# Four fused layers on one core: layer 2's scores four row strips at a time, layer 3's condition as a narrow product, one order for the whole program

## The chip, the cores and the metric

The kernel runs on one core of one Trainium2 chip, as a single launch. The metric is the device time of that launch in microseconds (us), lower is better. The core has five engines with a queue each: PE (matrix products and transposes), DVE (vector), ACT (scalar, exponentials), POOL (a second, slower vector engine) and SP (here it only starts transfers). Everything is float32. One float32 product shows in the trace as two MATMUL records, each with a LDWEIGHTS record of its own.

## The reference

Thirty-two batches of 128 tokens with 128 features pass through four layers, one after the other:

- Layer 0: adaptive layer norm, attention with 16 heads of 64, and a 512-wide MLP with GELU, both gated.
- Layer 1: RMS norm with FiLM, attention with one head of 128, and an MLP.
- Layer 2: adaptive layer norm, attention with 16 heads of 8, and an MLP, both gated.
- Layer 3: a graph attention. Its first product is what this change touches:

```
row_zero = v.sum(-1) == 0
q_exp = where(row_zero, 0, q[:, None, :])          # q: the condition of the batch, 128 numbers
self_feat = concat([v, q_exp], -1) @ W_self.T + b_self
for d in range(2):                                  # two directions, 16 heads of 8, keys: the first 20 nodes
    aff = (q_d . k_d) * scale, masked by adj, + label bias;  softmax;  weighted sum; output product
out = v + relu(output)
```

In layer 2, scores are `einsum('bqhd,bkhd->bhqk', Q, K)` with 8 features per head, softmax over the 128 keys.

## The kernel before

The 32 batches are worked in NG = 8 groups of G = 4 batches, so that a tile of 4 x 128 = 512 columns fills one of the eight PSUM banks. A group passes through four parts, each a Python generator that yields after every step: `front` (layer 0's attention, 76 steps), `mid` (layer 0's MLP and all of layer 1), `back` (layer 2) and `last` (layer 3). Each part has one set of SBUF tiles, so it works on one group at a time, while the other parts work on other groups. Every engine runs the same step lists and does its own share of each step.

What decides which step is next on an engine is a written order, `ORDERS`: a string of letters for each engine, one letter per step, made beforehand. `weave` walks the string and advances the generator of that letter. Before the change there are three orders: "head" (329 steps: groups 0 to 2 fill the pipeline), "steady" (170 steps, walked NG - 4 = 4 times, with the front of group it+3, mid of it+2, back of it+1 and last of it) and "tail" (348 steps: the remaining parts drain). PE's order also deals the banks: `Phase` walks it and gives each result that a step `begins` the bank that has been free longest; a bank is held from the step that begins the result to the step that lists it in `ends`. At run time PE waits on a semaphore until the bank's last reader is done.

The steps that the change touches:

- `S2` (layer 2, steps 0 to 7 of a group, two for each batch). The 16 heads of a batch are 4 units ("A", u), each a row strip: 32 of the 128 partitions hold the 8 features of 4 heads. The moving operand `km` holds the keys with the other heads' features set to zero, so one product of 32 rows, 128 columns of weights and 2 x 128 moving columns gives two heads. Step k computes units 2k and 2k+1 (line 1142), two strips into two banks. DVE then takes each unit's row maximum (line 1451), ACT the exponentials of unit 2k in `S2` and of 2k+1 in `E2` (line 947), and PE transposes the results in `T2` and `T2'` (line 1150). `V2` (line 1160) multiplies by the values, with four column strips side by side.
- `adj` (layer 3): PE transposes the edge sums of the second direction into a bank (line 1182); DVE copies the condition of the four batches from `condT` to `gcond` (line 1518), waits for that copy, and builds the mask and bias.
- `sum3`: PE sums the features of each token over the partitions (line 1017, weights `ones`); DVE turns this into `qx`: the condition where the sum is not zero, else 0, for 4 x 128 columns (line 1537).
- `self3`: PE computes `W_v x3 + W_q qx`, two 512-column products into one bank, the second of which waits for DVE's `qx`; DVE adds the bias (line 1381).

```
elif what == "self3":
    linear(P, "self3", [(w3[:, 0, :], x3T[:, :]), (w3[:, 1, :], qx)], after=["sum3"])
```

SP has its own hand-written sequence of waits and loads: the next group's input for the front (`load_norm`), the input again for the residual (`load_res`), the edge masks (`load_edges`, five transfers) and the stores.

Of the kernel before, what the change touches and what calls it, by code (L numbers as in the profile page):

```python
# [133 lines left out]
def end_steps():  # L134
    steps = [Step("adj", 0, ["adj"], ["adj"]), Step("sum3", 0, ["sum3"], ["sum3"]),
             Step("self3", 0, ["self3"], ["self3"]), Step("qk3", 0, ["q3_0", "q3_1", "k3"], ["q3_0", "q3_1", "k3"])]
    for s in range(NU3 + 5):
# [10 lines left out]
        if s < NU3:  # L148
# [8 lines left out]


STEPS = {"F": front_steps(), "M": mid_steps(), "B": back_steps(), "E": end_steps(), "A": front_steps(), "Q": front_steps(),
         "U": mid_steps(), "L": front_steps(False), "N": mid_steps(), "C": back_steps(), "D": back_steps(), "G": end_steps(),  # L160
         "H": end_steps(), "I": end_steps()}
STEP_NS = {"F": {"qk": 1720, "T": 440, "T'": 440, "S": 1000, "v": 900, "E": 300, "a": 1000, "I": 100, "stat": 300, "unit": 300, "turn": 450,
                 "o": 860, "y": 500},
           "M": {"stat": 1700, "unit": 1400, "turn": 1700, "up": 1900, "down": 1900, "back": 1500, "qk1": 1800, "v1": 1200,
                 "A1": 1500, "E1": 2500, "T1": 1000, "a1": 1200, "o1": 1500},
           "B": {"stat": 1700, "unit": 1400, "turn": 1700, "up": 1900, "down": 1900, "back": 1500, "kq2": 1900, "v2": 1200,
                 "S2": 1300, "T2": 1000, "T2'": 1000, "E2": 1000, "V2": 1300, "o2": 1800, "y2": 1500, "xt": 800},
           "E": {"adj": 1700,
                 "sum3": 1500, "self3": 1900, "qk3": 2500, "u3": 2000, "y3": 1500}}
STEP_NS.update({x: STEP_NS[kind] for kind, like in (("F", "AQL"), ("M", "UN"), ("B", "CD"), ("E", "GHI")) for x in like})  # L170

# [6 lines left out]
def edge_slot(i):  # L178
# [12 lines left out]
    "head": {  # L191
        "PE": (
            "AAAAAAAAAAAAAAAAAAAAAAAAAAAAAAAAAAAAAAAAAAAAAAAAAAAAAAAAAAAAAAAAAAAAAAAAAAAQAQUUQQQQUQQQQQQQQQUQUQQU"
            "UQQQUQQQUUQQUQQQQQUQQUUUQQQQQQQUQQUQQQQQQQUQQQUQQQQQUQQQUQUUQQQQQUQFFUQFQFQQQBQQQFQFFFFBFFFFMMFFMFBF"
            "FFFBMFBMBBMMBBBBFFBFBBFMFBFFFFFFBMBBMFBBFBMBFFBBFFFFBMBBFMMFFMFBFBMBFMBFFFMBBMFFBBBMFBBFFBFBFMFFFFBM"
            "BFBBFFBMFMFFBFFFFBFMFFFBFBFBB"),
        "DVE": (
            "AAAAAAAAAAAAAAAAAAAAAAAAAAAAAAAAAAAAAAAAAAAAAAAAAAAAAAAAAAAAAAAAAAAAAAAAAAAAQQUQQUQQQUQQUUUQQQQQQQQQ"
            "UQQQQUUQQQUQQUQQQUQUUQQQQQUQQQQQQQUQQQUQQUQQQUQQQUQUQUUQQQQQUQQQQQQQQFFUFQQQQQFQQFFFFFMBFMFFFBFFMMBF"
            "FFBFMBFBMFBFBBMBBBFFFMBBFMFFFFFBFBBFBMBBFBMBFBFBFFFMBFBBMMFBFFMBFFMBFMBBFFFMBMFBFBBBBFBMFBFFMFFBFFFB"  # L200
            "FFBBMFFMMBBFFFFBFFFFFBFBMFFBB"),
        "ACT": (
            "AAAAAAAAAAAAAAAAAAAAAAAAAAAAAAAAAAAAAAAAAAAAAAAAAAAAAAAAAAAAAAAAAAAAAAAAQQAQQQQQQAQQAAQQUQQUUUQUQQQQ"
            "QQQQUUQUQUQUQQQQQQUUQUUUQQQQUQQQQQQQQQQQQQQQUQQUQQUQQUQUQQUQUUUQQQQFQFQQFQQQFQBQQFFQFFFFMFFBBFMFFFFF"
            "FFMBMMBBBFFBBBBMBFFMFBBFFFFBFBBFFBFBFMBBBFFBMMFBFMFBFMMBBFMMFFBFBMFMMFFBFFBBBFBBFBFBBBMBFFMFMFFBFMMM"
            "FBFFFBFFFFFMBFFFFBFBFFBBFFBBB"),
        "POOL": (
            "AAAAAAAAAAAAAAAAAAAAAAAAAAAAAAAAAAAAAAAAAAAAAAAAAAAAAAAAAAAAAAAAAAAAAAAAAAAQQAQQUQQQQUUUUQQQQQQQQQQU"
            "UQUQQQQQQUQQQQQUUQUQQUUQUUQQUQQUQQQQQQQQQQQQQQQQUQQQUUUQQQQUFFQQQFQQQQFUQFQFFQQQQQQFUMBBMFMFMFMFMFBF"
            "FFBBBFBFFBBFBBFBFFMFBBMFBFFMFFFFFFFMBBMBBBBFFMFBBBFFBFFMMFFBFBFBBBMBMBFFMFBFBFFBFBBFMMBFMFBBFFFMFFFF"  # L210
            "BFFFBBBMFFMMFFBBFFFBMFFFFBBBB"),
    },
    "steady": {
        "PE": (
            "MFFFEBMFFFFBEBFBBMEBFFEBBBMEMEBBMFFBMFFEBFFBFFBMFFBFFBMBFFFBEBBFFFBFMFFBBEFBFBFMFEBFFFBMBMBMBFFMFFFF"
            "EBFMFFFFBMBEBBMFBFFFFBFFMFFFFBEMBFFBFFEMFFFFBMMBBFFFFBEBEMBMBFFBFBFEBE"),
        "DVE": (
            "MFBFMFBFBFEFFEFBBEBBMEBMEFMBBBMEFFFBBFMFBFEFFBFMFFBBFFBBBMFBFBFFBFEFFFFMEBFBBFFMFEBMFFFBBMBMBFFFMFMF"
            "BEFFEFFFFFBMBBMBFBFBFMFFBFFBFEFFMFFBFFMEFFFFMBEBFBMFFBFBMBMFFFEFBEBBBE"),
        "ACT": (  # L220
            "MBFEFFEBMMFFEEFBFBBFFEBFBBBMMBBFFFBFBFMFBMFBFBMEFFBFBFFMMFEFEBBBFFFFFFMBBBEFBFBFFEFFBFMBBBBFMFMFMFFF"
            "BEFMFFMFBBEBBBFMBFFMFFFFBFFFFFFBFEMMFBFEBFFFFMBMEEFMBEBBFBBFBFBFEMFBFF"),
        "POOL": (
            "MFEFEBBFFMBEFBBFFBMBFFEBBFBFFFBBFMEBFMFBFFBFBBEEBFFFFBMBMBMEFFMMBBBBFFBFFEFFBFFFFMFMBFBBFEFFFMMFMFFM"
            "BEBFFBEMFBBBFBFFFFMFFBBFBFFFFMFFFEFFFFFFEMMMMFFEEFFFBBFEFMEBFBBBBBBMBB"),
    },
    "tail": {
        "PE": (
            "BBLEMLLLLLLLBEMMBLBLBEBBBMEBMEBBLBMBLLLBMLELBLBLEMLBLMLBBBBELLBBEEBMBMBEBBEMLBLEMLLLMLBLELBLMLLLBLBM"
            "LBLMEBLBBLLLBMMLLLMBLEBLLLLEBLBBLLBMELLLLMBBLMBLBLLBBLMLLMLLLLCLLLLLCGGCGCCGNCNCNGCCGCNCNNCNGCCGNCCC"  # L230
            "NCCNNCCGNCCNCNGNCGCNCCNCCNGNCCCGCCGCCNCNGGCCGCNCNCCCCNNCGCCCCHDDDHDDDHDDHHDDDDHDDHDDDDDDDDHDHDDDDDDD"
            "DDHDDDDDDHDHDHDHDHDDHDDDHDDDDHIIIIIIIIIIIIIIIIII"),
        "DVE": (
            "BLBLMLEMLEBLLLMMLLBBBLBBEBBEMBEBBMLBBLLMLLEBLLBBLBELLLMMBBLBMEBLBEEBMBEBBBEMLLBELBBLLMMLLLLMELLEMLLB"
            "LLEBBBLBBBLMBLMLLMLMLBLLLLLEBBLBMLELBLLBLLLMBBLLLLBBLBMLMLLMLLLLLLLCGCGNCGCCGNCCNCGCNGCCCNCNNCGNCNCC"
            "CNCCGNCGCNCCGNNGNCNCGCCNCCNCCNGGCCCCNGCCCCNGCNGCCCCNCGCCNCCNCDDDHDHDDDHDDHDDHDDDHHDDDDDDDDHDHDDDDDDD"
            "DDDHDDDDHDHDDHHDDHDDHDDDHDHDDDIIIIIIIIIIIIIIIIII"),
        "ACT": (
            "BELMMLBEMLLLLLELBBLBLBBBBMMBEBEBBMBLEMLMMBLLMLBLELBLBEBLLBBLMLBLBEEBBBEBBBLEMBMMELLLLLMBBELLBLLLLMLL"
            "MMLBBLMLEBBBBLLLBLMLELBELBLLLBLBLEMLBLLLLBBMLBMBMBLLLLLLLBLMCLLLLLLLCGNGNCGGCCNCGGCCCNNCCCCNCNGCNCNC"  # L240
            "NCGCCGNCCNCCNNGGNCNCCCCNCCGCNNGCCGCNCCGCGCCCNNCCNGCCNCNGCCCCCDDDDDDDHHDDDHDDDHHHHDDHDDDDDDDDHDDDDDDD"
            "DDHDDDHDDDHDDHDDDDHDHHDDHDDDHDIIIIIIIIIIIIIIIIII"),
        "POOL": (
            "BBELMMLLELLLLBLLMMBBMLBBLBBBEMBBELBLMBBBBLBEEBBLBMLLEMBEBLLBMELLEBBBMLBEBMELLLELLMLLLLBLLBMBMLLMBBLE"
            "BLEMBMLLLBLMBLLLBMELLBBLLLBLLBBLMEMLBBMMLBLLLMLBLBLLLLLLLLLLLLLLBBCNNEGNGCGCCCCCCCGCCCGCCNNNCCGGNNNG"
            "NCCCGNNCNNCCCCGGNCNCCCCCNCNGNCCNGCCCGCCCGCCCCGCNCNCGNCNCCCNCDDGDDDDHHDHDHDHDDDDHDHDDDDDDDDHDHDDDDDDD"
            "DDHDDDDDDDHHDHHDDDDDDHHHDDDDDHIIIIIIIIIIIIIIIIII"),
# [8 lines left out]
def order_pairs():  # L256
# [18 lines left out]

    for a, b in ("AU", "UM", "QM", "UB", "LN", "MN", "MC", "BC", "ND", "CD", "EG", "BG", "GH", "CH", "HI", "DI"):
        follow(a, b)
# [25 lines left out]
class Phase:  # L303
# [3 lines left out]
    def __init__(self, banks, orders, turns=1, prefer=range(8)):  # L307
# [18 lines left out]
        for b in range(8):  # L326
            banks.dealt[b] += turns * self.per[b]
# [1334 lines left out]
```

## Time and the profile before

| | |
|---|---|
| median of 3 runs | 1239.77 us (1237.17 to 1240.85) |
| the profiled execution | 1240.78 us, of which the span from first to last instruction is 1239.0 us |
| mean granted PE clock | 0.946 of full |
| PE busy | 1110.0 us (90%) |
| DVE busy | 879.8 us (71%) |
| ACT busy | 772.8 us (62%) |
| POOL busy | 434.2 us (35%) |

A busy time is the union of the records of an engine. PE's two records for one product overlap their neighbours, so the mean duration of one is more than what it adds to the stream; the distance from start to start tells that. One pass of "steady" takes 134.6 us (a four-record product of line 1036 in the chain starts at 414.27, 548.90, 683.54 and 818.18 us).

### The profile page before, as it was taken

Reading aid. Unit: us, or ns where it says so; the run is one execution under the profiler, and the core shown is the slowest. Engines: PE = TensorE matmul, PEld = TensorE weight load, DVE = VectorE, ACT = ScalarE, POOL = GpSimd, SP = SyncE. Lnnn points to the kernel's source line nnn. Section 1 sums busy time; section 2 is a strip of 40 time slices with the busy share of each in tenths; the row PEclk is TensorE's granted clock in tenths of the full one; section 3 lists DMA queues with packets and bytes.
Section 4 is the critical chain, followed back from the end, with each engine's and each line's share of the span. In section 5 each row is a group of like instructions: output and inputs, shape, how many; then the busy total and the mean of one; then the engine's idle time right before and its main releaser. Section 6 shows DMA issues by size and latency. Waiting matters only on the chain.

```text
span 1239.0 us, 24134 instructions
## 1 busy us (share of the span) xinstructions
PE 1110.0 (90%) x8411; PEld 748.2 (60%) x8411; DVE 879.8 (71%) x2510; ACT 772.8 (62%) x2888; POOL 434.2 (35%) x599
## 2 busy tenths in 40 slices
PE   5889989989999999999999999998989977879865
PEld 4655755665567656775667656765666545646533
DVE  3456656775888688987799688877786478656655
ACT  1646557874688648873787468863866546726622
POOL 1322323332254333541445225432453234214313
PEclk9999999999999999999999999998979998886695
DMA  8000000001000100000000100010000100010000
GB/s 246 2 10 10 10 1 1 10 10 31 1 10 10 31 10 10 1 28 20 9 3 11 39 1 10 2 31 9 10 2 1 38 1 1 1 38 1 1 9 9
DMA packets 21822, 20.98 MB, mean 17 GB/s; under 512 B 1143, under 2 KB 20296, under 8 KB 21448
## 3 DMA queue, kind: packets, MB, share of 16 engines
q1 hardware_dynamic: 18536, 15.26, 4.4%
q10 hardware_dynamic: 3168, 4.19, 1.1%
q8 instruction: 69, 1.13, 0.4%
q14 instruction: 49, 0.40, 0.1%
HBM read 17.35 MB, written 2.10 MB: 16 GB/s over the span
## 4 chain that ended last, share of the span: by engine, by line
PE 63%; DVE 24%; ACT 7%; POOL 3%; issue 2%; DMA 1%; POOLq 0%; DVEq 0%; ACTq 0%
PE bank L1017 9%; PE bank L1036 7%; PE bank L1024 6%; PE bank L1142 5%; PE bank L1041 4%; PE bank L1074 4%; PE bank L1084 4%; PE bank L1150 3%; PE bank L1059 3%; PE bank L1068 3%; PE bank L1011 3%; PE bank L1232 2%; ACT prob_space L947 2%; PE bank L1221 2%; ACT fprobs L883 2%
## 5 line engine op out<-in xcount | busy, mean ns | idle before, releaser
L771 POOL TENSOR_TENSOR fprobs<-fprobs,frinv 128x512 f32<-128x512 f32 x128 | 132.4, 1039 | 282.5 <-DVE frinv L1327 282.2
L883 ACT ACTIVATE fprobs<-bank,fnegmax 128x128 f32<-128x128 f32 x512 | 180.8, 385 | 63.3 <-DVE fnegmax L1322 63.2
L947 ACT ACTIVATE prob_space<-bank,negmax 128x128 f32<-128x128 f32 x512 | 180.7, 380 | 22.2 <-DVE negmax L1451 21.9
L1017 PE MATMUL bank<-fhT,w_qkv 128*128 128x512 f32 x256 | 124.2, 607 | 1.6 <-DVE edge L1521 0.8
L883 ACT ACTIVATION_READ_ACCUMULATOR fprobs<-bank,fnegmax 128x1 f32 x512 | 115.6, 226 | 0.0
L947 ACT ACTIVATION_READ_ACCUMULATOR prob_space<-bank,negmax 128x1 f32 x512 | 113.4, 222 | 0.0
L1322 DVE TENSOR_REDUCE fnegmax<-bank 128x4 f32<-128x512 f32 x128 | 82.1, 682 | 43.7 <-PE bank L1059 43.7
L744 POOL TENSOR_TENSOR rstd<-veps,half 128x4 f32<-128x4 f32 x40 | 40.8, 1019 | 204.5 <-DVE veps L1284 184.3
L1451 DVE TENSOR_REDUCE negmax<-bank 128x4 f32<-128x512 f32 x128 | 82.3, 684 | 31.8 <-PE bank L1142 31.6
L889 ACT ACTIVATE fprobsT<-bank 128x512 f32<-128x512 f32 x128 | 74.4, 602 | 48.6 <-PE bank L1068 48.6
L1150 PE MATMUL bank<-ident,prob_space 128*128 128x128 f32 x512 | 86.3, 300 | 7.6 <-ACT prob_space L947 4.1
L953 ACT ACTIVATE prob_space<-bank 128x512 f32<-128x512 f32 x128 | 76.1, 609 | 26.8 <-PE bank L1150 26.7
L1068 PE MATMUL bank<-ident,fprobs 128*128 128x128 f32 x512 | 75.4, 278 | 17.3 <-POOL fprobs L771 14.8
L1068 PEld LDWEIGHTS bank<-ident,fprobs 128*128 128x128 f32 x512 | 58.7, 142 | 50.2 <-POOL fprobs L771 25.3
L894 ACT ACTIVATE fk<-bank 128x512 f32<-128x512 f32 x64 | 38.6, 603 | 73.2 <-PE bank L1017 72.7
L1142 PE MATMUL bank<-km,qk 32*128 32x256 f32 x512 | 80.9, 437 | 1.0 <-issue 0.8
L1150 PEld LDWEIGHTS bank<-ident,prob_space 128*128 128x128 f32 x512 | 63.4, 153 | 27.9 <-issue 19.8
L1059 PE MATMUL bank<-fk,fq 64*128 64x128 f32 x1024 | 75.2, 287 | 2.2 <-DVE fq L1332 1.6
L1024 PEld LDWEIGHTS bank<-w_qkv,fhT 128*128 128x128 f32 x512 | 64.9, 191 | 18.8 <-issue 16.5
L1059 PEld LDWEIGHTS bank<-fk,fq 64*128 64x128 f32 x1024 | 63.2, 189 | 19.0 <-issue 16.7
L1084 PE MATMUL bank<-fattnT,w_out 128*128 128x512 f32 x128 | 68.5, 617 | 5.6 <-DVE fattnT L1344 5.6
L801 POOL TENSOR_TENSOR adjw<-adjf,labels 80x176 f32<-80x176 f32 (+1 forms) x96 | 54.5, 568 | 52.3 <-ACT adjf L942 52.3
(193 smaller groups left out, 2499.0 us busy)
## 6 DMA issues: line engine op xcount, KB each, us to landing
adj<-in_mask_BxSxSx_ik SPq DMA_DIRECT2D x8, 440.0 KB
adj<-in_mask_BxSxSx_ik SPq DMA_DIRECT2D x32, 110.0 KB
x_norm<-in_x SPq DMA_DIRECT2D x8, 256.0 KB, 2.9
x_res<-in_x SPq DMA_DIRECT2D x8, 256.0 KB, 2.9
out<-x_out SPq DMA_DIRECT2D x8, 256.0 KB, 2.3
w_qkv<-in_L_cond_W_qkv ACTq DMA_DIRECT2D x1, 1536.0 KB, 7.0
prob_space<-in_w_mod SPq DMA_DIRECT2D x1, 1024.0 KB
w_up<-in_w_up ACTq DMA_DIRECT2D x1, 768.0 KB, 12.7
```

Source lines behind the costliest of these rows:

```text
L771: pool.tensor_tensor(p, p, wide(frinv[:, u, :], D), ALU.mult).then_inc(fnormed.sem, 1)
L883: ins = act.activation(fprobs[:, u % NP, b, :], P.bank(("S", u))[:, tok(b)], ACT.Exp, bias=fnegmax[:, u, b:b + 1], accum_out=frsum[:, u, b ...
L947: ins = act.activation(probs[:, u % NP, i, :], P.bank(("A", u))[:, tok(i)], ACT.Exp, bias=negmax[:, u, i:i + 1], accum_out=rsum[:, u, i:i ...
L1017: ins = pe.matmul(P.bank(result)[:, :], w, a, start=(i == 0), stop=(i == len(terms) - 1))
L1024: ins = pe.matmul(P.bank(result)[:, tok(b)], a[:, tok(b)], w, start=(i == 0), stop=(i == len(terms) - 1))
L1036: pe.matmul(P.bank(result)[:, :], w_up[:, l, tok(c)], part.hT[:, :], start=True, stop=True).then_inc(P.full_sem(result), 1)
L1059: ins = pe.matmul(P.bank(("S", 2 * c + r))[:, tok(b)], fq[rows, c % 2, tok(b)], fk[rows, c % 2, tok(b)], start=True, stop=True)
L1068: ins = pe.transpose(P.bank(("T", u))[:, tok(b)], fprobs[:, u % NP, b, :], ident[:, :])
L1084: ins = pe.matmul(P.bank("o0")[:, :], w_out[:, c, :], fattnT[:, c % 2, :], start=(c == 0), stop=(c == C0 - 1))
L1142: ins = pe.matmul(P.bank(("A", u))[:, tok(2 * n, 2)], qk[strip(u), 0, tok(b)], flat(km[strip(u), b % 2, 2 * n:2 * n + 2, :]), start=True, ...
L1150: ins = pe.transpose(P.bank(("T", u))[:, tok(i)], probs[:, u % NP, i, :], ident[:, :])
L1451: dve.tensor_reduce(negmax[:, u, :], P.bank(("A", u))[:, :].rearrange("p (i k) -> p i k", i=HS), AX.X, ALU.max, negate=True).then_inc(max2 ...
```

## The change

1. **Scores.** Step `S2` with even k computes all four units of the batch: four row strips into four banks, with the strips in the inner loop. Step `S2` with odd k issues nothing on PE. The step lists say so: an even step begins four results and the odd one none. DVE, ACT and POOL do the same as before.
2. **Condition.** In `adj`, PE also computes `W_q q` for the four batches, a product with 4 moving columns, into 4 spare columns of the same bank. DVE copies those to `gcond` in place of the copy from `condT`, and no longer waits between. `qx` now is that product where the token's sum is not zero. `self3` is one product on PE, and DVE adds bias and `qx` in one `scalar_tensor_tensor`.
3. **Order.** The three orders become one, "all", of 1357 steps per engine (as many as 329 + 4 x 170 + 348), with a letter for each part of each group (fronts A to H, mids I to P, backs Q to X, lasts a to h). `Phase` with its turns becomes `Plan`. SP walks DVE's order with small generators of its own. The explicit waits that go with it: PE waits for the turned input of the front before its first product (`ln0`), and DVE waits for the previous group's bias before it writes the first edge sums.

```
-            begins, ends = {"S2": ([("A", 2 * w), ("A", 2 * w + 1)], [("A", 2 * w)]),
+            begins, ends = {"S2": ([("A", 2 * w + j) for j in range(S4)] if w % 2 == 0 else [], [("A", 2 * w)]),
...
-                        b = k // 2
+
                         if k % 2 == 0:
+                            b, units = k // 2, range(2 * k, 2 * k + S4)
                             pe.wait_ge(*km_ready.nth(g, b))
-                        banks_free(P, drained=["q2"] if k == 0 else [], empty=[("A", u) for u in (2 * k, 2 * k + 1)])
-                        for n in range(2):
-                            for u in (2 * k, 2 * k + 1):
-                                ins = pe.matmul(P.bank(("A", u))[:, tok(2 * n, 2)], qk[strip(u), 0, tok(b)],
-                                                flat(km[strip(u), b % 2, 2 * n:2 * n + 2, :]), start=True, stop=True)
...
+                            banks_free(P, drained=["q2"] if k == 0 else [], empty=[("A", u) for u in units])
+                            for n in range(2):
+                                for u in units:
+                                    ins = pe.matmul(P.bank(("A", u))[:, tok(2 * n, 2)], qk[strip(u), 0, tok(b)],
+                                                    flat(km[strip(u), b % 2, 2 * n:2 * n + 2, :]), start=True, stop=True)
...
+                        ins = pe.matmul(P.bank("adj")[:, 2 * G * NK3:2 * G * NK3 + G], w3[:, 1, :], condT[:, 1, g * G:(g + 1) * G], start=True, stop=True)
...
-                        linear(P, "self3", [(w3[:, 0, :], x3T[:, :]), (w3[:, 1, :], qx)], after=["sum3"])
+                        linear(P, "self3", [(w3[:, 0, :], x3T[:, :])])
...
-                        dve.tensor_copy(gcond[:, :], condT[:, 1, bass.ds(g * G, G)]).then_inc(chain.sem, 1)
-                        dve.wait_ge(*chain.last(g))
                         dve.wait_ge(*P.full("adj"))
+                        dve.tensor_copy(gcond[:, :], P.bank("adj")[:, 2 * G * NK3:2 * G * NK3 + G])
...
-                        biased(P, "self3", sT[:, :], ROW["L3_cond_b_self"])
+                        c = ROW["L3_cond_b_self"]
+                        dve.wait_ge(*P.drained("sum3"))
+                        dve.wait_ge(*P.full("self3"))
+                        dve.scalar_tensor_tensor(sT[:, :], P.bank("self3")[:, :], col[:, c:c + 1], qx, ALU.add,
+                                                 ALU.add).then_inc(P.free_sem("self3"), 1)
...
                     if what == "qk":
+                        if c == 0 and g:
+
+                            pe.wait_ge(*plan.view(FRONTS[g - 1]).drained("ln0"))
...
+                    if p == 0 and g:
+
+                        dve.wait_ge(*bias_ready.nth(g - 1, 0))
...
+            def front(P, g):
+                for what, _, _, _ in STEPS[P.letter]:
+                    if what == "unit" and g + 2 < NG:
+                        sp.wait_ge(*fz_ready.nth(g + 1, 0))
+                        load_norm(g + 2)
+                    yield
```

SP's `mid` waits for "z0" and issues `load_res(g + 1)` in step "back"; its `back` waits for the last edge sum and issues `load_edges(g + 1)` at step EDGE_LAST; its `last` waits for "y3" and stores.

## Rows read from the trace of the kernel before

**Rows 1.** The page: span, busy times, PE's busy tenths and clock in 40 slices

```profile
span 1239.0 us, 24134 instructions
...
PE 1110.0 (90%) x8411; PEld 748.2 (60%) x8411; DVE 879.8 (71%) x2510; ACT 772.8 (62%) x2888; POOL 434.2 (35%) x599
...
PE   5889989989999999999999999998989977879865
...
PEclk9999999999999999999999999998979998886695
```

**Rows 2.** Windows: stretch, its length, then PE, PEld, DVE, ACT, POOL busy, clock

```profile
465.00:600.00 135.00, 130.09 (x1048) 88.14 (x1048) 110.43 (x313) 95.35 (x361) 53.44 (x73) 1.00 0.05 14
...
1000.00:1100.00 100.00, 85.20 (x601) 56.19 (x600) 68.91 (x202) 58.83 (x207) 35.36 (x55) 0.87 0.05 13
1100.00:1200.00 100.00, 79.75 (x503) 51.72 (x504) 62.03 (x176) 51.56 (x189) 30.85 (x54) 0.74 0.01 4
```

**Rows 3.** The page: the chain that ended last, shares by engine

```profile
PE 63%; DVE 24%; ACT 7%; POOL 3%; issue 2%; DMA 1%; POOLq 0%; DVEq 0%; ACTq 0%
```

**Rows 4.** Waits of PE from 414 to 549 us, first and last of nine

```profile
PE bank L1017 <- DVE edge L1521: 1.2, 1, 1.2
...
PE bank L1011 <- ACT p3T L988: 0.2, 1, 0.2
```

**Rows 5.** Timeline of PE: the first records of one S2 step, all, the next

```profile
606.57 0.48 PE L1142 MATMUL bank<-km,qk 32*128 32x256 f32 x2
...
606.57 1.13 PE L1142 MATMUL bank<-km,qk 32*128 32x256 f32 x8
607.63 1.98 PE L1041 MATMUL bank<-mhid,w_down 128*128 128x512 f32 x4
```

**Rows 6.** Groups by line and shape: products and readers around the scores

```profile
L947 ACT ACTIVATE prob_space<-bank,negmax 128x128 f32<-128x128 f32 x512 | 180.7, 380 | 22.2 <-DVE negmax L1451 21.9
...
L947 ACT ACTIVATION_READ_ACCUMULATOR prob_space<-bank,negmax 128x1 f32 x512 | 113.4, 222 | 0.0
...
L1142 PE MATMUL bank<-km,qk 32*128 32x256 f32 x512 | 80.9, 437 | 1.0 <-issue 0.8
...
L1160 PE MATMUL bank<-prob_space,vm 128*32 128x128 f32 x1024 | 38.9, 298 | 0.0
```

**Rows 7.** Windows of line 1142 alone: stretch, length, PE and PEld busy, clock

```profile
0.00:1000.00 1000.00, 55.23 (x384) 33.39 (x384) 0.99 0.07 19
1000.00:1239.00 239.00, 25.62 (x128) 14.92 (x128) 0.78 0.03 8
```

**Rows 8.** Windows: the score stretch of one pass, and one in the tail

```profile
600.00:680.00 80.00, 77.15 (x729) 55.90 (x728) 70.10 (x185) 66.24 (x273) 38.23 (x51) 1.00 0.03 8
...
1121.00:1163.00 42.00, 40.05 (x259) 28.48 (x257) 25.62 (x63) 29.68 (x128) 15.12 (x26) 0.51 0.01 1
```

**Rows 9.** Groups by line and shape: condition, sum3 and self3

```profile
L1250 PE MATMUL bank<-condT,prob_space 128*128 128x32 f32 x32 | 7.0, 402 | 1.1 <-DVE condT L1593 1.1
...
L1017 PE MATMUL bank<-q,w 128*128 128x512 f32 x16 | 8.5, 610 | 0.0
...
L1581 DVE SCALAR_TENSOR_TENSOR q<-bank,bout,sT 128x256 f32<-128x256 f32 x16 | 7.4, 464 | 9.5 <-PE bank L1213 9.5
...
L1381 DVE TENSOR_SCALAR sT<-bank,col 128x512 f32<-128x512 f32 x8 | 6.0, 750 | 5.4 <-PE bank L1017 5.4
...
L1518 DVE COPY gcond<-condT 128x4 f32<-128x4 f32 x8 | 1.3, 159 | 0.1
```

**Rows 10.** Waits of PE from 1000 us to the end: the one for qx

```profile
PE bank L1017 <- DVE q L1537: 1.8, 1, 1.8
```

**Rows 11.** Groups by shape, then the page: DVE's first use of the front's input, its load

```profile
L1272 DVE BATCH_NORM_STATS2 stats<-x_norm 128x6 f32<-128x128 f32 x32 | 6.8, 275 | 8.6 <-DMA x_norm<-in_x 8.6
...
x_norm<-in_x SPq DMA_DIRECT2D x8, 256.0 KB, 2.9
```

More of the change, by code:

```diff
@@ L153, in end_steps @@
     return steps
[L159 to L170, printed above, removed]
+FRONTS, MIDS, BACKS, ENDS = "ABCDEFGH", "IJKLMNOP", "QRSTUVWX", "abcdefgh"
+STEPS = {}
+for _g in range(NG):
+    STEPS.update({FRONTS[_g]: front_steps(_g + 1 < NG), MIDS[_g]: mid_steps(), BACKS[_g]: back_steps(), ENDS[_g]: end_steps()})
 NPIECES = 12
@@ L213 @@
[L213 to L247, printed above, removed]
@@ L300, with __init__ @@
         assert not order_faults(_order), (_name, order_faults(_order))
-class Phase:
-    def __init__(self, banks, orders, turns=1, prefer=range(8)):
+class Plan:
+    def __init__(self, banks, orders, prefer):
         self.banks, self.orders = banks, orders
         order = orders["PE"]
-        self.base = list(banks.dealt)
         starts = {x: [p for p, y in enumerate(order) if y == x] for x in set(order)}
@@ L384, in __init__ @@
         self.free_sems = [ctx.enter_context(nc.semaphore(f"bank{i}_free")) for i in range(8)]
-        self.dealt = [0] * 8
 class Count:
@@ L413, with weave @@
 BACK_LINKS = 5
-END_LINKS = 12
+END_LINKS = 11
 Part = namedtuple("Part", "z hT yT hid gmod stat norm0 var_ready rstd_ready z_ready chain")
-def weave(order, **streams):
+def weave(order, streams):
     for letter in order:
@@ L565, in build @@
         ps = banks.ps
-        head = Phase(banks, ORDERS["head"], prefer=(0, 1, 4, 5, 6, 7, 2, 3))
-        steady = Phase(banks, ORDERS["steady"], NG - 4)
-        tail = Phase(banks, ORDERS["tail"])
-        assert all(head.at["A", r][0] not in (2, 3) for r in ("q_0", "k_0", "v_0"))
+        plan = Plan(banks, ORDERS["all"], prefer=(0, 1, 4, 5, 6, 7, 2, 3))
+        assert all(plan.at["A", r][0] not in (2, 3) for r in ("q_0", "k_0", "v_0"))
         w_qkv_in = sem("w_qkv_in")
@@ L643, in strip, with run @@
             return slice(32 * (u % S4), 32 * (u % S4) + 32)
+        def run(name, prologue, front, mid, back, last):
+            prologue()
+            streams = {}
+            for letters, stream in ((FRONTS, front), (MIDS, mid), (BACKS, back), (ENDS, last)):
+                streams.update({letter: stream(plan.view(letter), g) for g, letter in enumerate(letters)})
+            weave(plan.orders["DVE" if name == "SP" else name], streams)
         block = ctx.enter_context(nc.Block())
@@ L679, in _ @@
             load_edges(0)
-            for g in range(2):
-                sp.wait_ge(*fz_ready.nth(g, 0))
-                load_norm(g + 1)
-            for g, mid_letter in enumerate("UM"):
-                sp.wait_ge(*head.view(mid_letter, 0).drained("z0"))
-                load_res(g + 1)
-                sp.wait_ge(*fz_ready.nth(g + 2, 0))
-                load_norm(g + 3)
-            sp.wait_ge(*adj_summed.nth(0, NPIECES - 1))
-            load_edges(1)
-            def steady_loads(it, norm):
-                sp.wait_ge(*steady.view("M", it).drained("z0"))
-                load_res(it + 3)
-                if norm is not None:
-                    sp.wait_ge(*fz_ready.nth(it + 4, 0))
-                    load_norm(norm)
-                sp.wait_ge(*adj_summed.nth(it + 1, NPIECES - 1))
-                load_edges(it + 2)
-                store(steady.view("E", it), it)
@@ L701, in _ @@
-            for it in range(NG - 4):
-                steady_loads(it, it + 5 if it + 5 < NG else None)
-            sp.wait_ge(*tail.view("M", 0).drained("z0"))
-            load_res(NG - 1)
-            sp.wait_ge(*adj_summed.nth(NG - 3, NPIECES - 1))
-            load_edges(NG - 2)
-            store(tail.view("E", 0), NG - 4)
-            sp.wait_ge(*adj_summed.nth(NG - 2, NPIECES - 1))
-            load_edges(NG - 1)
-            for i, letter in enumerate("GHI"):
-                store(tail.view(letter, 0), NG - 3 + i)
+            sp.wait_ge(*fz_ready.nth(0, 0))
@@ new lines, in _, with mid @@
+            load_norm(1)
+            def front(P, g):
[4 more added lines that the diff above has]
+                    yield
+            def mid(P, g):
+                for what, _, _, _ in STEPS[P.letter]:
+                    if what == "back" and g + 1 < NG:
+                        sp.wait_ge(*P.drained("z0"))
+                        load_res(g + 1)
+                    yield
@@ new lines, in back, with last @@
+            def back(P, g):
+                for i in range(len(STEPS[P.letter])):
+                    if i == EDGE_LAST and g + 1 < NG:
+                        sp.wait_ge(*adj_summed.nth(g, NPIECES - 1))
+                        load_edges(g + 1)
+                    yield
+            def last(P, g):
+                for what, _, _, _ in STEPS[P.letter]:
+                    if what == "y3":
+                        store(P, g)
+                    yield
+            run("SP", lambda: None, front, mid, back, last)
@@ L715, in build @@
         NWEIGHTS = 5
-        def run(name, prologue, front, mid, back, last):
-            prologue()
-            weave(head.orders[name], A=front(head.view("A", 0), 0), Q=front(head.view("Q", 0), 1), F=front(head.view("F", 0), 2),
-                  U=mid(head.view("U", 0), 0), M=mid(head.view("M", 0), 1), B=back(head.view("B", 0), 0))
-            for it in range(NG - 4):
-                weave(steady.orders[name], F=front(steady.view("F", it), it + 3), M=mid(steady.view("M", it), it + 2),
-                      B=back(steady.view("B", it), it + 1), E=last(steady.view("E", it), it))
-            weave(tail.orders[name], L=front(tail.view("L", 0), NG - 1), M=mid(tail.view("M", 0), NG - 2),
-                  N=mid(tail.view("N", 0), NG - 1), B=back(tail.view("B", 0), NG - 3), C=back(tail.view("C", 0), NG - 2),
-                  D=back(tail.view("D", 0), NG - 1), E=last(tail.view("E", 0), NG - 4), G=last(tail.view("G", 0), NG - 3),
-                  H=last(tail.view("H", 0), NG - 2), I=last(tail.view("I", 0), NG - 1))
         @block.gpsimd
@@ L1052, in front @@
                     elif what == "S":
-                        if c == 0 and P.letter == "A":
+                        if c == 0 and g == 0:
                             pe.wait_ge(setup_done, 1)
@@ L1080, in front @@
                     elif what == "o":
-                        if c == 0 and P.letter == "A":
+                        if c == 0 and g == 0:
                             pe.wait_ge(weights_in, 16 * NWEIGHTS)
@@ L1497, in back @@
                         dve.wait_ge(*P.drained("xt"))
-                        if P.phase is not head:
+                        if g:
                             dve.wait_ge(*rel_ready.nth(g - 1, 1))
```

167 lines of the change are left out of this document (102 added, 65 removed).

## Prediction

> **What bounds the kernel now.** I read the page first, then windows, the chain, and PE's waits, and only then single lines. The page shows PE busy 90% of the span, and its row of tenths stands at 9 from slice 9 to slice 28 [rows 1]. The reader is to see in it two regimes. In the middle PE is the bound: in 135 us of one steady pass it is busy 130.09, with DVE at 110.43 and ACT at 95.35, all at full clock [rows 2], and over a pass its waits are nine small ones from 1.2 down to 0.2 us [rows 4]. After 1000 us PE is busy 85.2 and 79.8 of 100 at clocks of 0.87 and 0.74 [rows 2]. There the chain goes through PE and DVE in turn; over the whole span it is PE 63%, DVE 24%, ACT 7% [rows 3]. So PE time removed before 1000 us should come off the end, unless DVE or ACT run out of room, and after 1000 us only part of it.
>
> **Scores.** One S2 step has 8 records. Two strips start together. The first pair ends 0.48 us after the start and the eighth record 1.13 us after it, so each of the three later pairs adds (1.13 - 0.48) / 3 = 0.22 us; the next instruction starts 1.06 us after the step's start [rows 5]. That is 4 rounds of 0.22 (0.87) and 0.19 us for filling and changing shape. The new step has 16 records: still 2 halves times 2 records = 4 rounds, if four strips run side by side. V2 does that with four column strips: its 1024 records are 32 steps of 32, in 38.9 us, 1.2 us a step or 0.15 us a round of four, for 128 moving columns, clocks mixed [rows 6]. That is the nearest row for four at once; row strips are seen only in twos. So the new step should cost what the old one cost, about 1.06 us, and there are 32 of them in place of 64. At full overlap half of line 1142's busy time goes: 55.23 / 2 = 27.6 us before 1000 us, 25.62 / 2 = 12.8 us after [rows 7]. The other bound is that only two strips overlap: 8 rounds, 8 x 0.22 + 0.19 = 1.92 against 2 x 1.06 = 2.12 us, 0.2 us for each of 32 batches, 6.4 us in all. I take full overlap.
>
> The Trainium skill has a figure for this ("TensorE: Matmul & The Clock Gate", Part 3, "Measured speedup vs the span model"): four row strips of 32 ran 3.07 times as fast as one after the other, not 4. By it a round of four would take 4 x 0.22 / 3.07 = 0.29 us and a step 1.34 us, an estimate from that page and rows 5; the saving would be 0.78 us a batch in place of 1.06, and the time some 7 us above my forecast. No row here has four row strips.
>
> How much of it reaches the end? The units are read while they are made: a row maximum on DVE and, on ACT, 4 exponentials of 380 ns and 4 reads of 222 ns, 2.4 us a unit [rows 6]. In the 80 us in which a steady pass has its scores, PE is busy 77.15 and DVE 70.10 [rows 8]. Without 4 x 1.06 PE has 72.9, and DVE is as full as PE. If PE keeps its idle 2.85 us, the stretch takes 75.8 us with DVE at 92%; if DVE can't be packed beyond its present 88%, it takes 80 and nothing is gained in it. Between these ends I take three quarters, nearer the first, since parts of a pass outside it leave DVE and ACT room that a new order can use (110.43 and 95.35 of 135 [rows 2]). In the tail the stretch from 1121 to 1163 us is PE at half clock, busy 40.05 of 42 [rows 8], and gives nearly all, but others give less: three quarters again. Scores: 0.75 x (27.6 + 12.8) = 30.3 us.
>
> **Condition.** The second product of self3 is the row `q,w`: 16 records, 8.5 us busy [rows 9]. Three quarters of it: 6.4 us. PE's wait for `qx`, 1.8 us once [rows 10], also goes, since the product no longer reads it. The narrow product is not in the trace. It adds 16 records with 128 columns of weights and 4 moving ones; the nearest row is the setup's product with 32 moving columns, 32 records in 7.0 us, 0.22 each, so 3.5 us above and nothing below; I take 2 us, as the shorter stream and the full clock make it less. On DVE the copy of 159 ns stays, from a bank now [rows 9], and one wait between two DVE instructions goes, under 0.1 us x 8 against a copy from a bank that may be slower by as much: nothing. The fused add reads a bank and SBUF: the row of the same kind takes 464 ns for 256 elements, so at most 928 for 512, against 750 now [rows 9]; that is 0.2 us x 8 = 1.4 us of DVE above and nothing below, behind PE's other work. I take nothing. If that cover is gone (the last group, where sum3, self3 and qk3 follow each other), it is 0.2 us once.
>
> **Order.** I walked both PE orders by the dealing rule that the code gives. The shape is the same: front g+3 over mid g+2, back g+1 and last g. The last front starts 28 steps earlier (983 against 1011 of 1357) and ends 6 later (1182 against 1176). Behind its end lie 142 us of PE work before and 126 after, counted with step lengths from the trace at full clock; shorter scores and self3 explain 11 of the 16, so 5 us of work move ahead of the thin tail. Up to 5 us could be gained by that. Against it, banks are tighter: of 1303 banks dealt a second time or more, 24 are taken within two steps of the holder's last step, where before no distance was under 3; score banks now go down to 2, before to 4. I take nothing, with 10 us either way. The new wait of PE for `ln0` has at least 7 other steps between the turn and the product in the new order; everything behind it on PE would wait, but over 4 us of other work lies between: nothing. DVE's wait for its own earlier bias lies behind work that its order has already put first: nothing. SP issues the same 8 + 8 + 40 loads and 8 stores. In its new sequence load_norm is issued at a unit step, over 80 steps before the stat step that reads it, and load_res comes over 80 steps before its reader, against 2.9 us from issue to landing; the only visible wait of DVE for a load is 8.6 us at the start [rows 11]. A store's wait for ACT delays what is queued behind it on SP (a load_res, a load_norm, edges), by a few of those steps: nothing.
>
> **Sum.** 1240.8 - 30.3 - 6.4 - 1.8 + 2.0 = 1204.3 for an execution like the profiled one. That one lies 1.0 above the median, so 1203.
>
> **Rivals.**
>
> *The readers fill up (0.20).* DVE at 88% of the score stretch [rows 8] takes PE's place and the scores pass only a quarter: 10.1 in place of 30.3, 1223 us. For it: 70.10 against 72.9. Against it: DVE has 135 - 110.43 = 25 us free in a pass [rows 2], most of it outside the score stretch. The Trainium skill warns of this ("TensorEngine Tiling (Array Packing)", "PSUM Bottleneck"): after a fourfold faster product the evacuation may be the bottleneck. The trace agrees that DVE is close, no more.
>
> *Bank waits (0.10), the other side.* Four banks are claimed at one point of PE's queue, so PE stands until the slowest of four readers is done, with fronts and mids queued behind it. The price is one unit's exponentials, 2.4 us [rows 6], for each of 32 batches: 77 us, and the time 1203 + 77 = 1280. It turns the sign from (30.3 + 6.4 + 1.8 - 2.0) / 32 = 1.1 us a batch on. For it: the distances above. Against it: they average 6.4 steps, 6.6 before in a steady pass, and line 1142 waited 1.0 us in all [rows 6].
>
> *Only two strips overlap (0.06).* 0.75 x 6.4 = 4.8 in place of 30.3: 1229. V2 speaks against it.
>
> *The tail's clock (0.08 better, 0.06 worse).* After 1000 us the mean clock on line 1142's window row is 0.78 [rows 7], so about 2 x 0.22 x 239 = 105 us ran at 1.2 GHz in place of 2.4. From 1121 to 1163 that was so although PE was busy 40 of 42 us, with strips and transposes [rows 8]; the 40 us of work would be 20. If the clock holds there, 20 us more come off: 1183. If less work on PE leaves more idle time and 40 us more run at half clock at the tail's 80% busy, 16 us go back: 1219. I see nothing that fixes the direction.
>
> **Chances and range.** The forecast has 0.50, with its own range 1190 to 1216: all of the scores and self3 pass (12 us less), or half of them (12 more). With the readers, the two strips and both clock cases the range reaches from 1175 to 1234, which leaves out the bank waits and the ends of others. A measurement of this kernel tells 0.3% (3.7 us) from no change. Faster by more than that: 0.50 + 0.20 + 0.06 + 0.14, less 0.02 for their upper ends: 0.88. Within it: 0.04. Slower: 0.08.
>
> **What would show it.** Line 1142's counterpart keeps 512 records in 32 steps of 16, rounds of four 0.22 us apart, busy about 40 us (two strips only: over 70). The row with `q,w` is gone, its counterpart with 4 moving columns is under 3.5 us. PE's busy time falls to about 1062. PE in the middle stays over 95% busy: if it falls to 90% with DVE over 85%, the readers were the limit; if its idle time stands before the score products or other products and ends on ACT's exponentials, it was the banks. A steady pass (front to front) takes 130 us or a little less. The prediction fails if passes stay at 134, or if the clock after 1000 us moves by more than 0.1.

## The result and the profile after

The changed kernel takes 1205.36 us (median of 4 runs, 1205.02 to 1207.95) against 1240.31 us of the kernel before beside it: a ratio of 0.9721, 95% interval 0.9690 to 0.9752. The forecast was 1203 us. The total came out; its parts did not, and most of this section and the next is about that.

The page of the changed kernel, the lines that answer to [rows 1] and [rows 3]:

```profile
span 1203.8 us, 24116 instructions
...
PE 1060.0 (88%) x8411; PEld 716.9 (60%) x8411; DVE 878.9 (73%) x2510; ACT 777.0 (65%) x2892; POOL 434.0 (36%) x599
...
PE   5899999899989989989899989899879988787675
...
PEclk9999999999999999999999999999989998998895
...
PE 51%; DVE 25%; ACT 17%; issue 3%; POOL 3%; DMA 1%; POOLq 0%; DVEq 0%; ACTq 0%
```

PE's busy time fell by 50.0 us, the span by 35.2 us, so PE idles 14.8 us more than before. The chain says what it idles for: PE's share went from 63% to 51% and ACT's from 7% to 17%.

Groups by line and shape, the ones that answer to [rows 6] and [rows 9]:

```profile
L1131 PE MATMUL bank<-km,qk 32*128 32x256 f32 x512 | 40.0, 428 | 14.3 <-ACT prob_space L932 3.9 <-issue 2.4 <-DVE p L1567 1.7
...
L1002 PE MATMUL bank<-x3T,w 128*128 128x512 f32 x16 | 9.2, 658 | 0.0
...
L1536 DVE SCALAR_TENSOR_TENSOR sT<-bank,col,q 128x512 f32<-128x512 f32 x8 | 6.0, 745 | 0.3 <-DVE vm L1466 0.2
...
L1173 PE MATMUL bank<-condT,w 128*128 128x4 f32 x16 | 2.6, 232 | 0.0
...
L1513 DVE COPY gcond<-bank 128x4 f32<-128x4 f32 x8 | 1.2, 152 | 0.3
```

The scores' 512 records are busy 40.0 us where they were busy 80.9 [rows 6]. The narrow product is 2.6 us. The fused add takes 745 ns, like the bias alone before. And before the score products PE now stands 14.3 us where it stood 1.0.

One step in the timeline of PE, answering to [rows 5]:

```profile
448.78 1.15 PE L1131 MATMUL bank<-km,qk 32*128 32x256 f32 x16
449.86 1.16 PE L1047 MATMUL bank<-fk,fq 64*128 64x128 f32 x16
```

Sixteen records from 448.78 to the next start at 449.86: 1.08 us, against 1.06 for eight.

Where along the span the time went shows in windows cut at the first product of the fourth front and of the last one (columns as in [rows 2]). Of the changed kernel:

```profile
0.00:285.00 285.00, 257.44 (x1895) 175.77 (x1896) 174.45 (x510) 177.52 (x674) 85.04 (x101) 0.99 0.12 36
285.00:811.00 526.00, 484.02 (x4025) 329.35 (x4023) 423.22 (x1207) 370.57 (x1416) 208.98 (x287) 0.99 0.04 12
811.00:1204.00 393.00, 318.57 (x2496) 211.74 (x2494) 281.25 (x794) 228.91 (x804) 139.99 (x211) 0.90 0.04 12
```

The same three stretches of the kernel before:

```profile
0.00:303.00 303.00, 263.24 (x1897) 178.72 (x1898) 175.64 (x511) 177.53 (x674) 85.17 (x101) 0.99 0.11 34
303.00:842.00 539.00, 518.91 (x4185) 352.00 (x4184) 440.42 (x1249) 379.40 (x1439) 213.77 (x292) 1.00 0.05 13
842.00:1239.00 397.00, 327.81 (x2332) 217.47 (x2330) 263.76 (x751) 215.86 (x775) 135.29 (x206) 0.84 0.04 10
```

So 18 of the 35 us are gained before the fourth front starts, 13 in the four passes, 4 behind. In the passes PE was busy 96% and is now busy 92%: 34.9 us of work went from this stretch and 13 us of time. Not all of that work is gone: the stretch has 160 records fewer and the last one 164 more, since the last front starts earlier in the order. A pass takes 526 / 4 = 131.5 us in place of 134.6.

The clock moved too, which the sum of the forecast took at nothing. Over the whole span its mean is 0.962, before 0.946. By an estimate from these two means, 2 x 0.038 x 1203.8 = 91 us ran at 1.2 GHz in place of 2.4, where 2 x 0.054 x 1239.0 = 134 us did before. Executions of one program differ in this as well: the old orders in the new code (below) took 1232.6 us in one execution at a mean clock of 0.954 and 1244.0 us in another at 0.941, 9 us for 0.01. At that rate some 14 of the 35 us came together with the clock, an estimate that is rather high, since a part of the removed work had itself run at the slow clock. Whether the change raised the clock, no run separates.

### The profile page after: what moved, and what is told of

It is laid out like the page before. It is cut to its first block, busy times and chain, and to the rows that moved or that the text cites. A ratio compares the mean times of both kernels' runs of the same rounds, so it can differ in the third digit from the quotient of the medians.

```text
span 1203.8 us, 24116 instructions
## 1 busy us (share of the span) xinstructions
PE 1060.0 (88%) x8411; PEld 716.9 (60%) x8411; DVE 878.9 (73%) x2510; ACT 777.0 (65%) x2892; POOL 434.0 (36%) x599
## 4 chain that ended last, share of the span: by engine, by line
PE 51%; DVE 25%; ACT 17%; issue 3%; POOL 3%; DMA 1%; POOLq 0%; DVEq 0%; ACTq 0%
PE bank L1002 8%; ACT prob_space L932 6%; PE bank L1009 6%; PE bank L1021 6%; PE bank L1047 4%; PE bank L1072 4%; PE bank L1026 4%; PE bank L1062 4%; ACT fprobs L868 3%; PE bank L1056 3%; PE bank L996 2%; PE bank L1149 2%; DVE negmax L1445 2%; PE bank L1139 2%; PE bank L1223 2%
## 5 line engine op out<-in xcount | busy, mean ns | idle before, releaser
L1002 PE MATMUL bank<-fhT,w_qkv 128*128 128x512 f32 x256 | 126.7, 616 | 4.8 <-ACT fprobs L868 2.4
L932 ACT ACTIVATION_READ_ACCUMULATOR prob_space<-bank,negmax 128x1 f32 x512 | 116.4, 228 | 0.0
L1139 PE MATMUL bank<-ident,prob_space 128*128 128x128 f32 x512 | 81.3, 291 | 15.0 <-ACT prob_space L932 9.2
L1056 PEld LDWEIGHTS bank<-ident,fprobs 128*128 128x128 f32 x512 | 58.6, 142 | 38.9 <-issue 19.6
L1139 PEld LDWEIGHTS bank<-ident,prob_space 128*128 128x128 f32 x512 | 60.5, 148 | 33.9 <-issue 22.5
L838 POOL TENSOR_TENSOR p<-p,rinv 128x320 f32<-128x320 f32 x64 | 46.9, 733 | 80.3 <-DVE rinv L1554 80.3
L1062 PE MATMUL bank<-fprobsT,fv 128*64 128x128 f32 x1024 | 71.7, 283 | 2.3 <-issue 1.0
```

Source lines behind the costliest of these rows:

```text
L932: ins = act.activation(probs[:, u % NP, i, :], P.bank(("A", u))[:, tok(i)], ACT.Exp, bias=negmax[:, u, i:i + 1], accum_out=rsum[:, u, i:i ...
L1002: ins = pe.matmul(P.bank(result)[:, :], w, a, start=(i == 0), stop=(i == len(terms) - 1))
L1056: ins = pe.transpose(P.bank(("T", u))[:, tok(b)], fprobs[:, u % NP, b, :], ident[:, :])
L1062: ins = pe.matmul(P.bank(f"a_{c}")[r * DH0:(r + 1) * DH0, tok(b)], fv[:, c % 4, b, r * DH0:(r + 1) * DH0], fprobsT[:, (2 * c + r) % NP, b, ...
L1139: ins = pe.transpose(P.bank(("T", u))[:, tok(i)], probs[:, u % NP, i, :], ident[:, :])
```

## The experiments

Costs below are differences of ratios (each to the kernel before on the same chip) times 1240 us, since the kernel before itself varies from chip to chip. The intervals of these ratios reach 3 to 5 us to either side, so a difference of two is known to about 6 us. A cost measured so also contains what the clock did; the mean clock of the profiled execution is given where it differs.

### Was it the four strips?

**Two pairs in one step.**

```
-for n in range(2):
-    for u in units:
+for pair in (units[:2], units[2:]):
+    for n in range(2):
+        for u in pair:
```

> The changed kernel, with the same steps, order and banks; only the four strips of a batch now run as two pairs, one after the other. PE gets 4 rounds of 0.216 us per batch back, 32 x 0.86 = 27.7 us at full clock. If PE is still what bounds most of the span and three quarters pass (my theory): 1226 us (1221 to 1232). If the readers of the scores, DVE and ACT, took over (rival): under 10 us slower, below 1215 us.

1209.15 us, ratio 0.9741 (0.9696 to 0.9785), not to be told from the changed kernel. That would have spoken for the rival, but the edit had not done what it said. Timeline of this kernel's PE:

```profile
449.74 1.16 PE L1132 MATMUL bank<-km,qk 32*128 32x256 f32 x16
450.83 0.94 PE L1047 MATMUL bank<-fk,fq 64*128 64x128 f32 x12
```

The sixteen records still take 1.09 us, and line 1132 is busy 39.3 us in all. The second pair, written behind all of the first, runs beside it. The run says nothing on what PE time is worth.

**Two pairs kept apart.**

```
+if pair == units[2:]:
+    pe.matmul(P.bank(("A", units[3]))[:, 0:4], ident[:, :], ident[:, 0:4], start=True, stop=True)
```

> The earlier run with the strips as two pairs left PE as it was: the second pair started 0.02 us behind the first, since nothing stood between them. Here a product with the full array and 4 moving columns stands between the two pairs, so that they really run one after the other; steps, order and banks stay. A step should take 2 x 1.06 + 0.2 = 2.3 us in place of 1.08, PE gets 32 x 1.2 = 39 us at full clock. If three quarters pass (my theory): 1205 + 29 = 1234 us, 1225 to 1243. If DVE and ACT are the limit: below 1217 us.

1226.03 us, ratio 0.9903 (0.9871 to 0.9935): 22.6 us slower than the changed kernel. Now the pairs are one behind the other:

```profile
452.42 1.13 PE L1134 MATMUL bank<-km,qk 32*128 32x256 f32 x8
453.48 0.39 PE L1131 MATMUL bank<-ident 128*128 128x4 f32 x2
453.79 1.13 PE L1134 MATMUL bank<-km,qk 32*128 32x256 f32 x8
454.85 1.16 PE L1047 MATMUL bank<-fk,fq 64*128 64x128 f32 x16
```

2.43 us a batch in place of 1.08. The page has PE busy 1108.2 us, 48.2 more, so 0.47 of the PE time reaches the end (0.35 to 0.6 with the 6 us above). The time lies at the low end of what my theory allowed (1225 to 1243), but the share lies below its three quarters and above the rival's 0.3. The clock is 0.953 here and 0.962 in the changed kernel; by the 9 us for 0.01 above, an estimated 8 of the 23 us came with it.

### What is the condition part worth, and why?

**The whole part undone.** The second product, its wait and the copy from `condT` back; the narrow product away.

```
-linear(P, "self3", [(w3[:, 0, :], x3T[:, :])])
+linear(P, "self3", [(w3[:, 0, :], x3T[:, :]), (w3[:, 1, :], qx)], after=["sum3"])
...
-dve.tensor_copy(gcond[:, :], P.bank("adj")[:, 2 * G * NK3:2 * G * NK3 + G])
+dve.tensor_copy(gcond[:, :], condT[:, 1, bass.ds(g * G, G)]).then_inc(chain.sem, 1)
```

> The changed kernel with the condition part undone: self3 is two 512-column products again, the second after DVE's qx, and the narrow product is gone. PE busy time goes up by 8.5 - 2.6 = 5.9 us, and the wait for qx comes back. My theory (three quarters pass, plus a wait of about 2 us): 6 us slower, 1211 us. Rival (hidden, since PE now has 144 us idle): within 2 us of the changed kernel.

1224.26 us, ratio 0.9880 (0.9836 to 0.9924): 20 us slower, three times the forecast (5 of them, by the same estimate, with a clock of 0.956). Two further runs take its halves, and one gives the part to the old orders.

**Only the wait.**

```
-linear(P, "self3", [(w3[:, 0, :], x3T[:, :])])
+linear(P, "self3", [(w3[:, 0, :], x3T[:, :])], after=["sum3"])
```

> The changed kernel, where only the wait of self3 for DVE's qx is put back and the second product stays away (the product doesn't need the wait). The run with the whole condition part undone was 19 us slower, not 6. If the wait is the cause, because the new order puts self3 closer behind sum3: 1215 to 1222 us. If the second product's PE time is the cause: within 2 us of the changed kernel.

1213.38 us, ratio 0.9804 (0.9769 to 0.9839): 10 us, below the 1215 to 1222 that I gave to the wait as the cause and far above the 2 us of the other case. Waits of PE in this run, the second largest group:

```profile
PE bank L1002 <- DVE q L1530: 11.8, 5, 5.0
```

Before the change this wait came once, for 1.8 us [rows 10]. In the new order, which was made without it, it comes five times and takes 11.8 us.

**Only the product.**

```
+linear(P, "self3", [(w3[:, 1, :], x3T[:, :]), (w3[:, 0, :], x3T[:, :])])
```

> The changed kernel with a second 512-column product in self3 (from x3T in place of qx, so without the wait; the sum is another one). If PE's time is what counts, 16 records and about 7 us of PE at three quarters: 1210 us. If the 19 us of the undone condition part were PE's time: 1220 us or more. If PE has room there: under 1207 us.

1212.43 us, ratio 0.9790 (0.9755 to 0.9824): 9 us, for 11.2 us more of PE busy time (1071.2). It lies nearest to the 1210 of "PE's time counts". The halves add up to the whole within what is known of each: 10 + 9 against 20.

**The new condition part alone, in the old orders.** The scores as before, and the three old orders written out as one:

```
-ORDERS["all"] = the new strings
+ORDERS["all"] = head + 4 x steady + tail of the kernel before, with the letters of the groups
```

> The old orders and the old scores with the new condition part alone. My prediction's terms for it: 6.4 + 1.8 - 2.0 = 6 us faster than the kernel before, 1234 us. Rival: it is worth the 19 us that undoing it cost, 1221 us; or, with the old order's 5 to 7 us of other work between sum3 and self3, only the PE time, 1236 us.

1227.61 us, ratio 0.9923 (0.9894 to 0.9952): 10 us faster than the kernel before (6 to 13 by the interval), between my 1234 and the rival's 1221. PE busy is 1097.4, 12.6 less. The windows (same cuts as above) put most of the gain behind the last front's start:

```profile
0.00:303.00 303.00, 263.51 (x1898) 179.29 (x1899) 175.75 (x512) 177.63 (x674) 85.16 (x101) 0.99 0.11 34
303.00:838.00 535.00, 516.13 (x4185) 351.46 (x4184) 440.14 (x1251) 379.56 (x1440) 213.78 (x292) 1.00 0.05 13
838.00:1225.00 387.00, 317.78 (x2330) 211.37 (x2328) 262.31 (x750) 215.27 (x775) 135.51 (x206) 0.85 0.04 10
```

Four passes give 4 us, 1 us each, for 2.8 us less of PE. The last stretch gives 10 (397 to 387), and PE is busy 10.0 us less in it with the same number of records (2330, before 2332). Four products of 1.06 us (8.5 / 8) against narrow ones account for 3 to 4 us of that at full clock. The clock is 0.85 there in place of 0.84, which gives a part of the rest; how the rest splits is open.

### What is the order worth?

**The old orders in the new code.** The same edit of `ORDERS`, with old scores and old condition.

> The kernel before in the code of the one after: old orders joined end to end with group letters, old scores, old condition; new are only SP's generators, the two explicit waits and the dealing of banks without a restart at the borders. My theory: nothing, 1240 us within 3 us. Rival: the new waits or SP's sequence cost or give something, more than 4 us either way.

1241.24 us, ratio 1.0003 (0.9966 to 1.0040). SP's generators, the explicit waits and the dealing without a restart cost nothing that shows.

**The new order with PE's old work.** A first try joined the two-pair edit (`for pair in (units[:2], units[2:])`) with the undone condition:

> Both of the edits above together: PE's work of the kernel before, in the new order and with the new banks. If the parts add, 1205 + 21 + 6 = 1232 us, and what is left to 1240 us, 8 us, is the order's. If the order is worth nothing (my prediction), it comes out at 1237 to 1243 us. If it comes out above 1245 us, the new order alone costs time and the products pay for it.

1224.14 us, ratio 0.9871 (0.9829 to 0.9913), the same as with the condition undone alone. Since the pairs overlap, it is that experiment again, and its reading of the order falls. With the pairs kept apart by the small product:

> New order and banks with PE's old work: the pairs of strips kept apart by a small product (its 0.2 us a batch is 6 us of PE that the kernel before hasn't), and the condition part undone. If the single costs add (21 + 19): 1245 us, and so the order alone is worth -5 to +1 us against the kernel before. If PE's waits of the two hide one another: 1232 to 1238 us.

1237.77 us, ratio 0.9980 (0.9953 to 1.0007), with PE busy 1116.8. That is 32 us above the changed kernel, where the single costs add to 23 + 20 = 43: the two hide one another in part, and each alone, measured by undoing it, counts some of the other's. Against the run with only the condition part undone, keeping the pairs apart costs 12 us for 45.8 us more of PE (1116.8 against 1071.0), a share of 0.27 in place of 0.47. Its windows, of an execution 4 us longer than the median:

```profile
0.00:286.00 286.00, 262.92 (x1906) 180.35 (x1907) 175.40 (x513) 177.67 (x674) 85.18 (x101) 0.99 0.12 36
286.00:830.00 544.00, 508.30 (x4053) 345.55 (x4052) 423.54 (x1207) 372.74 (x1416) 209.44 (x287) 0.99 0.04 11
830.00:1240.00 410.00, 345.60 (x2518) 230.32 (x2517) 281.71 (x793) 229.97 (x803) 139.64 (x211) 0.88 0.04 12
```

The head's 17 us are there with PE's old work (286 against 303): they are the order's. This execution gives them back in the passes (544 against 539) and the last stretch (410 against 397), which has more of the work now. In the passes PE idles 36 us where it idled 20, and 9.4 us of that are four waits for `qx`, which this order does not space out.

**The four strips in the old orders.** With the new condition part, and four strips at once in every group but group 5: with it too, the old orders make the engines wait for one another for good.

```
-BACKS[_g]: back_steps()
+BACKS[_g]: back_steps(_g in (0, 1, 2, 3, 4, 6, 7))
```

> Old orders joined, new condition part, and the four strips at once in seven of the eight groups (group 5 keeps two and two; 28 of 32 batches). Against the old orders with the condition part alone (1227.6 us) PE has 28 x 1.05 = 29 us less. If an old order can use it at three quarters: 1206 us. If the freed time mostly turns into waits because each engine's order was made for two units at a time (rival: the order is what lets the scores pay): 1215 us or more. If below 1205 us, the new order is worth nothing or costs.

1263.08 us, ratio 1.0199 (1.0156 to 1.0242): 34 us slower than the same orders without the four strips, and slower than the kernel before. PE did its part. The page:

```profile
PE 1073.8 (85%) x8411; PEld 725.8 (58%) x8411; DVE 875.2 (69%) x2510; ACT 775.0 (62%) x2888; POOL 435.3 (35%) x599
```

PE's waits from 310 to 876 us:

```profile
PE bank L1077 <- DVE p L1574: 12.6, 4, 3.1
PE bank L1007 <- DVE mhT L1295: 6.8, 4, 1.7
PE bank L1138 <- DVE fq L1330: 5.4, 4, 1.4
```

And the windows of the passes and of what follows:

```profile
310.00:876.00 566.00, 509.57 (x4186) 347.20 (x4185) 436.53 (x1250) 380.88 (x1440) 213.91 (x292) 0.98 0.05 12
876.00:1260.00 384.00, 304.15 (x2330) 202.48 (x2328) 262.87 (x750) 215.57 (x775) 136.15 (x206) 0.87 0.04 10
```

PE busy is 23.6 us less than without the strips (1097.4) and the span 35 us more (1260.0 against 1225.0): PE idles 58.6 us more, 2.1 us for each of 28 batches. The reader is to see that little of it stands at the score products themselves:

```profile
L1138 PE MATMUL bank<-km,qk 32*128 32x256 f32 x512 | 44.6, 426 | 15.2 <-DVE fq L1330 5.4 <-ACT prob_space L937 4.0 <-ACT fprobs L873 2.4
```

That is 15.2 us, about as much as the 14.3 in the changed kernel. PE waits four times, once a pass, at the front's output product (line 1077) for a DVE instruction of layer 3, at a mid product for `mhT`, and so on. My reading is that what is queued behind a late bank on one engine makes the next engine late; the run does not show which bank. The passes take 566 us where they took 535.

### What limits the changed kernel?

**Less DVE.**

```
-P.bank(("A", u))[:, :].rearrange("p (i k) -> p i k", i=HS)
+P.bank(("A", u))[:, :].rearrange("p (i k) -> p i k", i=HS)[:, :, 0:D // 2]
```

> The changed kernel with the row maximum of layer 2's scores taken over half of the keys: DVE has 128 x 0.3 us = 40 us less (the softmax is scaled by another number). If DVE is what the scores' freed PE time ran into: 8 to 20 us faster, 1185 to 1197 us. If PE and ACT are the limit: within 4 us of the changed kernel, over 1201 us.

1193.57 us, ratio 0.9630 (0.9594 to 0.9666): 11 us faster for 34.4 us less of DVE (844.5 us busy), 0.33 of it. That is inside the 1185 to 1197 of "DVE is what the time ran into".

**Less ACT.**

```
+kept = {"accum_out": rsum[:, u, i:i + 1]} if i % 2 == 0 else {}
```

> The changed kernel where the exponentials of two of the four heads of a unit in layer 2 don't sum (their row sums are 1): 256 reads of the accumulator at 228 ns go, 57 us of ACT. If ACT's chain of exponentials is the limit (its share of the chain rose from 7% to 17%): 15 to 30 us faster, 1175 to 1190 us. If DVE or PE: within 5 us, over 1200 us.

1196.41 us, ratio 0.9662 (0.9623 to 0.9702): 7 us faster for 22.6 us less of ACT (754.4 us busy, before 777.0), 0.32 of it. I had counted the 58 us of the reads. Their own row did fall so, from 116.4 to 57.2 us, but a busy time counts overlapping records once, and most of a read lies beside another record of ACT. The time lies between the two forecasts. So ACT is not the limit alone, and DVE counts without being it alone: PE's time passes at 0.47, DVE's at 0.33, ACT's at 0.32. The 6 us leave the last two wide, 0.2 to 0.5 for DVE and from near nothing to 0.6 for ACT.

## Why the prediction was right, and where it was not

- **The new score step.** Right. Four rounds of 0.22 us, 1.08 us in place of 1.06, busy 40.0 against the forecast 40. The bound of 6.4 us and the rival "only two strips overlap" fall. The figure of the Trainium skill that I quoted ("TensorE: Matmul & The Clock Gate", "Measured speedup vs the span model", for 512 moving columns) would have given 1.34 us a step, by my estimate; with the 256 columns here the measurement decides for 1.08.
- **Three quarters of it reach the end.** This step failed. Measured by undoing it, 0.47 of PE's time passes: 0.47 x 40.9 us = 19 us in place of 30.3. With the condition part undone as well it is 0.27, close to the quarter of the rival "the readers fill up". I had the marker for it: PE over 95% busy in the passes; it is at 92%. The rival's own sign, DVE over 85% busy there, did not come: it is 423 of 526 us, 80%. Less work on DVE or on ACT does shorten the kernel, each at about a third, so the readers take part. None is the limit by itself, which my either-or between two bounds had no room for.
- **The condition part, 6 us.** Mis-sized. It is worth 10 us in the old orders (6 to 13, so my figure is at the edge) and 20 us in the new one. I took the wait for `qx` as the 1.8 us that the profile of before shows [rows 10]; but that was a wait that its order had spaced out. What the edit removes is the order's duty to space it: put back into the new order, which does not space it, the wait alone is 10 us. The product's PE time passed at 0.8 (9 of 11.2 us, the 9 known to 6), about as I took it, but 11.2 us is more than the row's 8.5. The narrow product (2.0 against 2.6 us) and the fused add (nothing) were right.
- **The order, nothing.** Right as a sum at old work (0.9980, the interval touches 1), wrong as a statement on the change. It gains 17 us in the head, where fronts 0 and 1 now overlap (front 1's first product starts at 80 us, before at 89) and PE idles 28 us there in place of 40; with PE's old work it loses about as much later; and it is what keeps the four strips from costing 34 us. Whether the tighter banks that I counted against it cost anything, no run separates.
- **Bank waits, 2.4 us a batch.** In the changed kernel, no: 14.3 us before the score products, 0.4 us a batch. In the old orders PE idles 2.1 us a batch more, near the rival's price, but not where the rival had it: at the score products it is 15.2 us in all. That the change would have cost time without its third part is shown; that it was by PE standing for the slowest of four readers is not.
- **The tail's clock.** The mean over the last 237 us is 0.86 where it was 0.78 [rows 7], inside the 0.1 that I allowed. The sum took this at nothing, which was too little. Over the whole span 43 us less ran at half clock, and I had priced 40 us of that at 16. So the rival "the clock holds" came in part: by the two estimates some 14 to 17 of the measured 35 us, which the other terms then cannot claim for themselves. That less work on PE caused this is not shown; the runs with more PE work have 0.87 and 0.88 from the last front on, with 0.90 in the changed kernel.

That the forecast of 1203 was so near is luck in good part: the terms erred in both directions, 11 us too much for the scores, 4 to 14 too little for the condition, and the clock, taken at nothing, moved the forecast's way and is contained in both measured costs. What stays open is the clock's cause, and how the order's share splits between the earlier overlap of fronts and the spacing of the four units; no run separates them.

## What to carry to other kernels

Where a written order keeps PE 96% busy, a wait that the profile barely shows may have been bought by placement. Its size in the old trace (1.8 us here) is then a low price for the dependency, and what it costs when put back into an order made without it (10 us) a high one. A change in how many buffers a step claims at once needs its order with it; the same edit was 34 us slower in the old order. Here, with three engines at 88, 73 and 65%, a quarter to a half of PE's time and about a third of the others' reached the end, not all from the busiest. And look at the clock of the two kernels before their times are divided among the parts of a change.

## What the runs showed of the hardware

Four row strips of 32 into four banks run fully side by side: 16 records in 1.08 us, 8 in 1.06. They do so also when the second pair of strips is written behind the whole of the first (1.09 us); with a small product on the full array between them they ran one after the other (2.43 us). That product also wrote into the bank of the last strip, so its shape and its bank are not separated. So the order in which strips are written did not matter in the one other order that was run, and what stood between them did.
